# Two attention layers: copies of the turned weights shared out anew, and the split context kept in DRAM for the second layer

## What is computed

```python
x = x + _L0_xattn_ref(_layernorm(x), ctx_1024, ...)             # 16 heads of 16, biases
x = x + _L0_ffn_ref(_layernorm(x), ...)                         # top 2 of 8 experts
x = x + _L1_xattn_ref(_layernorm(x), ctx_1024, ..., mask)       # same context, other weights, a mask
x = x + _L1_ffn_ref(_layernorm(x), ...)
...
q = (x @ w_q).heads; k, v = (ctx @ w_kv).heads
out = softmax(q @ k.T * scale) @ v @ w_out
```

## Time and profile before

| | us |
|---|---|
| median of 3 timed runs | 782.3 |
| lowest, highest | 781.62, 786.86 |
| profiled execution | 776.57 |
| its span | 774.5 |

### The profile page before, as it was taken

One profiled execution on the slowest core, in us unless ns is written; L12 is line 12 of the kernel. 1 busy time (PEld: TensorE's weight loads), 2 busy tenths in 40 slices (PEclk: granted clock), 3 DMA queues, 4 the chain that ended last, 5 costly groups with the idle time before them and its releaser, 6 DMA issues. The chain is left out here.

```text
span 774.5 us, 14634 instructions
## 1 busy us (share of the span) xinstructions
PE 571.8 (74%) x5357; PEld 482.4 (62%) x5357; DVE 413.5 (53%) x1210; ACT 356.3 (46%) x816; POOL 147.8 (19%) x210
## 2 busy tenths in 40 slices
PE   4798999998448009999999940588889988827643
PEld 3676777776327009989899930476677777715432
DVE  3677677677421701343233253466656566648785
ACT  2676666666220004232232321357777777744520
POOL 1132333332100260000000055022323323100000
PEclk9899999999756558999999985789999999976978
DMA  5100000000198255554554213200000000000001
GB/s 150 58 15 8 22 22 2 2 1 2 31 347 270 86 186 204 184 198 154 187 191 157 75 58 106 88 22 22 8 16 21 2 2 2 2 2 1 0 1 47
DMA packets 38938, 57.11 MB, mean 74 GB/s; under 512 B 4410, under 2 KB 32083, under 8 KB 38740
## 3 DMA queue, kind: packets, MB, share of 16 engines
q1 hardware_dynamic: 37332, 52.50, 21.2%
q0 software_dynamic: 1536, 3.67, 1.5%
HBM read 47.91 MB, written 8.26 MB: 73 GB/s over the span
## 5 line engine op out<-in xcount | busy, mean ns | idle before, releaser
L788 PE MATMUL a_ring<-ident,a_e 112*125 112x112 f32 x768 | 102.2, 284 | 3.0 <-ACT a_e L411 3.0
L788 PEld LDWEIGHTS a_ring<-ident,a_e 112*125 112x125 f32 x768 | 90.7, 192 | 19.9 <-issue 14.8
L1118 ACT ACTIVATE ex_h_t<-ex_h,b_e 128x128 f32<-128x128 f32 x168 | 48.0, 369 | 97.9 <-PE ex_h L1370 97.9
L577 DVE CUSTOM_DVE_ANT_0 a_e<-a_s,a_mask 112x375 f32<-112x375 f32 x128 | 65.2, 542 | 39.3 <-issue 21.9
L1370 PE MATMUL ex_h<-ex_xg_t,w_s 128*128 128x128 f32 x672 | 80.9, 280 | 0.1
L1370 PEld LDWEIGHTS ex_h<-ex_xg_t,w_s 128*128 128x128 f32 x672 | 79.1, 197 | 0.5 <-DVE ex_xg_t L1265 0.5
L570 DVE TENSOR_REDUCE a_mx<-a_s 112x2 f32<-112x750 f32 x64 | 59.7, 933 | 32.7 <-PE a_s L779 32.7
L419 ACT ACTIVATE a_et<-a_ring 125x448 f32<-125x448 f32 x96 | 51.5, 536 | 53.1 <-PE a_ring L788 53.1
L411 ACT ACTIVATE a_e<-a_e,a_shift 112x375 f32<-112x375 f32 x128 | 70.4, 599 | 11.9 <-DVE a_shift L582 11.1
L1382 PE MATMUL ex_y<-w_s,ex_h_t 128*128 128x256 f32 x336 | 75.8, 379 | 0.0
L411 ACT ACTIVATE a_e<-a_s,a_shift 112x375 f32<-112x375 f32 x128 | 66.4, 571 | 12.5 <-DVE a_shift L582 12.2
(11 more groups left out here) (253 smaller groups left out, 849.9 us busy)
## 6 DMA issues: line engine op xcount, KB each, us to landing
w_s<-in_L_ffn_W SPq DMA_DIRECT2D x21, 1024.0 KB, 5.0
w_all<-in_L_ffn_W SPq DMA_DIRECT2D x8, 1024.0 KB, 11.9
a_ctx<-in_ctx SPq DMA_DIRECT2D x16, 375.0 KB
x_slots<-ex_zeros SPq DMA_DIRECT2D x1, 2688.0 KB
ex_xg<-x_slots SPq DMA_DIRECT2D x21, 128.0 KB, 4.9
y_slots<-ex_y_sb SPq DMA_DIRECT2D x21, 128.0 KB, 1.7
b_all<-in_L_ffn_b SPq DMA_DIRECT2D x1, 1024.0 KB
wu<-in_L_ffn_w SPq DMA_DIRECT2D x1, 1024.0 KB, 5.9
```

The source lines that it names most:

```text
L577: ins = v.tensor_tensor_reduce(out=es[:, t % 2, r, 0:SK], in0=s[0:S, r * 512:r * 512 + SK], in1=mask_sb[:], scale=1.0, scalar=-3.0e38, op0 ...
L788: last = nc.tensor.transpose(bank("et", t, kc)[0:KP, r * S:(r + 1) * S], es[:, t % 2, r, kc * KP:(kc + 1) * KP], ident[0:S, 0:S])
L1118: last = a.activation(h_t[:, i % 2, f], hb[i % 2][:, f * 128:(f + 1) * 128], ACT.Gelu, bias=b1_e[:, i % 2, f:f + 1])
```

## The change

1. In both layers ScalarE copies pieces 0 and 1 one after the other, ahead of all exponentials of the pass; VectorE copies piece 2. (Line numbers of the changed kernel are higher by 1 to 37.)
2. In layer one SyncE stores each batch's split context, 752 KB, into a new DRAM tensor `ct_dram` (`keep_context`), once the split is done; the load of batch b+3 stands behind it in SyncE's program. GpSimd's split of the next batch waits for that store.
3. Layer two no longer loads, turns, copies or splits the context. GpSimd issues a load of the kept split (`load_turned`) into one of two buffers of `a_ct`: batches 0 and 1 at the start of the layer, batch b+2 in its pass g3. The units `ct` leave the ring. Keys and values wait for the load.

```diff
+    ct_dram = nc.dram_tensor("ct_dram", (B, 128, 2 * DC * SKP), F32)
...
+                ct_bufs = 1 if first else 2
+                ct_all = sb(f"{tag}_ct", [128, ct_bufs, 2, DC, SKP], F32R)
...
+                order = [u for u in order if first or u[0] != "ct"]
...
+                        def keep_context(b):
+                            if b:
+                                sp.wait_ge(ct_lo, 2 * b)
+                            else:
+                                wait_read(sp, "ct", 0, 0)
+                                wait_read(sp, "ct", 0, 1)
+                                sp.wait_ge(filled, 3)
+                            sp.dma_start(ct_dram[b], ct_all[:, 0].rearrange("p i c n -> p (i c n)").bitcast(F32)).then_inc(ct_kept, 16)
...
-                        load_ctx(1)
-                        load_ctx(2)
-                        for b in range(B - 3):
-                            wait_filled(sp, "ct", b, 1)
-                            load_ctx(b + 3)
+                        if first:
+                            load_ctx(1)
+                            load_ctx(2)
+                            for b in range(B):
+                                keep_context(b)
+                                if b + 3 < B:
+                                    load_ctx(b + 3)
+                            sp.wait_ge(ct_kept, 16 * B)
...
                             wait_filled(pool, "v", b - 1, 1)
-                            g_.tensor_copy(ct[:, 0, c, 0:SK], ct_raw[:, c]).then_inc(ct_hi, 1)
+                            pool.wait_ge(ct_kept, 16 * b)
+                            g_.tensor_copy(ct_all[:, 0, 0, c, 0:SK], ct_raw[:, c]).then_inc(ct_hi, 1)
...
+                        def load_turned(b):
+                            if b >= 2:
+                                wait_filled(pool, "k", b - 2, 1)
+                                wait_filled(pool, "v", b - 2, 1)
+                            g_.dma_start(ct_all[:, b % 2].rearrange("p i c n -> p (i c n)"), ct_dram[b].bitcast(F32R))\
+                                .then_inc(ctx_in[b % 2], 16)
+
+                        if not first:
+                            load_turned(0)
+                            load_turned(1)
...
                             if g == 3 and b + 2 < B:
-                                context(b + 2, 0)
-                                context(b + 2, 1)
+                                if first:
+                                    context(b + 2, 0)
+                                    context(b + 2, 1)
+                                elif b >= 0:
+                                    load_turned(b + 2)
...
                             if 0 <= t < NQ:
                                 turned(t, 0)
+                                turned(t, 1)
                             if t + 1 < NQ:
                                 exps(t + 1, 0)
-                            if 0 <= t < NQ and mask is not None:
-                                turned(t, 2)
-                            if t + 1 < NQ:
                                 exps(t + 1, 1)
...
                             if 0 <= t < NQ:
-                                turned(t, 1)
-                                if mask is None:
-                                    turned(t, 2)
+                                turned(t, 2)
...
                         def wait_context(b):
-                            if b:
+                            if not first:
+                                pe.wait_ge(ctx_in[b % 2], 16 * (b // 2 + 1))
+                            elif b:
                                 pe.wait_ge(ct_lo, 2 * b)
```

More of the change, by code:

```diff
@@ L115, in attention_layer @@
                 k_raw = sb(f"{tag}_k_raw", [128, DC, SKP])
-                ctx_sb = sb(f"{tag}_ctx", [KP, 3, KC, D])
-                ct = sb(f"{tag}_ct", [128, 2, DC, SKP], F32R)
-                ct_raw = sb(f"{tag}_ct_raw", [128, DC, SK])
+                first = x_from is not None
+                if first:
+                    ctx_sb = sb(f"{tag}_ctx", [KP, 3, KC, D])
+                    ct_raw = sb(f"{tag}_ct_raw", [128, DC, SK])
+                ct_bufs = 1 if first else 2
+                ct_all = sb(f"{tag}_ct", [128, ct_bufs, 2, DC, SKP], F32R)
                 vx = sb(f"{tag}_v", [KP, 2, KC, H, 32])
@@ L156, in attention_layer @@
                 w_in = [sem(f"{tag}_w_in{i}") for i in range(4)]
-                ctx_in = [sem(f"{tag}_ctx_in{i}") for i in range(3)]
+                ctx_in = [sem(f"{tag}_ctx_in{i}") for i in range(3 if first else 2)]
+                ct_kept = sem(f"{tag}_ct_kept")
                 filled = sem(f"{tag}_filled")
@@ L351, in context @@
                             if b == 0:
-                                a.activation(ct[:, 0, c, 0:SK], bank("ct", b, c)[:, 0:SK], ACT.Copy).then_inc(ct_first, 1)
+                                a.activation(ct_all[:, 0, 0, c, 0:SK], bank("ct", b, c)[:, 0:SK], ACT.Copy).then_inc(ct_first, 1)
                                 return
@@ L439, in _ @@
                             weight(1, 0)
-                        act.wait_ge(filled, 3)
-                        context(0, 0)
-                        context(0, 1)
+                        act.wait_ge(filled, 3 if first else 2)
+                        if first:
+                            context(0, 0)
+                            context(0, 1)
                         if not transposed:
@@ L483, in _ @@
                                     keys(b + 1, 1)
-                            if g == 3 and b + 2 < B:
+                            if g == 3 and b + 2 < B and first:
                                 context(b + 2, 0)
@@ L531, in first_context @@
                             dve.wait_ge(ct_first, c + 1)
-                            v.tensor_tensor(ct[:, 1, c, 0:SK], bank("ct", 0, c)[:, 0:SK], ct[:, 0, c, 0:SK].bitcast(F32),
+                            v.tensor_tensor(ct_all[:, 0, 1, c, 0:SK], bank("ct", 0, c)[:, 0:SK], ct_all[:, 0, 0, c, 0:SK].bitcast(F32),
                                             ALU.subtract).then_inc(is_read("ct", 0, c), 1)
@@ L620, in _ @@
                         normal(0)
-                        first_context(0)
-                        first_context(1)
+                        if first:
+                            first_context(0)
+                            first_context(1)
                         if not transposed:
@@ L878, in _ @@
                             if g == 3:
-                                if b + 2 < B:
+                                if b + 2 < B and first:
                                     context(b + 2, 0)
```

9 lines of the change are left out of this document (6 added, 3 removed).

## The result

The changed kernel takes 739.3 us (median of 4 runs, 735.4 to 741.0); the kernel before, on the same chip, 782.0 us. The ratio is 0.944 (95%: 0.938 to 0.951). The profiled execution took 735.4, its span is 733.4 us, 41.1 less than the 774.5 of the earlier trace rows.

The account below looks back on a forecast made before the run. Steps were taken as bound by waits for four PSUM banks, the loop through ScalarE's exponentials, and TensorE's program order in layer two. Layer one -7.3, layer two -3.0, -7.0 and -11.0 sum to -28.3: median 754.0 us, 8-in-10 range 745 to 770.

Parts of the forecast that it names:

- Start of layer two: Layer two's keys start earlier without the context's turn and split, -3.9; weights landing 0.9 later make it -3.0 us.
- Wait for the load: Layer two's values wait 0.5 us per batch for the kept context, taken to land 5.05 us after issue.
- The cover of 4.55: Time in layer two between issue of the kept-context load and the values wanting it: 4.55 us.
- The forecast's case without a wait: Layer two's kept-context load takes an estimated 3.8 us, so values do not wait and the total is 2.5 us less.
- g1: Second of a batch's four score steps: 4.75 us forecast in layer one, 4.68 in layer two without a bank wait.
- Rival 1: Layer two's kept-context load lands late: 766 us in all, or 780 if it lands at 9.3; chance 0.18.
- Rival 3: Layer two's kept-context loads crawl at 60 GB/s, making the kernel slower than before: 816 us; chance 0.04.
- Steady batches of layer one: Five layer-one batches from 75 to 180 us: each 19.95 us against 21.15 through fewer bank waits, -6.0 in all.
- rival 2: ScalarE's longer loop takes layer one's gain: 774 us, or 761 if only the gain vanishes; chance 0.08.
- light steps: Layer one's four end steps without bank waits, which pay for ScalarE's loop of 4.64 us: +1.3 in all.
- First steps: Steps before the steady batches: layer one's seven -2.6 us; layer two's -7.0, with bounds of -3.5 and -8.
- Rival 4: The copies do not free banks as claimed, leaving only the removed context work, about -15: 767 us; chance 0.08.

Follow-up runs that it names:

- second execution: The changed kernel run and profiled again without an edit: 739.5 us, ratio 0.948 to the kernel before; profiled span 737.9 us.
- query_weights_first: The kernel before, with layer two's query weights load issued ahead of the context's instead of behind it: 777.7 us, ratio 0.997.
- context_ahead: The changed kernel, with one raw context of 375 KB loaded into an unread tile ahead of layer two's query weights: 747.0 us, ratio 0.960.
- split_context: The changed kernel, with each context load of layer one in two pieces of 112 and 13 partitions: 738.6 us, ratio 0.949.
- late_load: The changed kernel, with the six loads inside layer two's steps issued later, behind the scores of the next step: 760.2 us, ratio 0.969.
- copy_between: The changed kernel, with ScalarE's copy of piece 1 in layer one moved between its two pairs of exponentials: 750.5 us, ratio 0.961.
- copies_only: The kernel before, with the copies dealt out as in the changed kernel in both layers and nothing kept in DRAM: 757.9 us, ratio 0.968.

## Why the prediction was wrong, and where it was right

The forecast of 754.0 had the mechanisms of both parts right and sized several terms too small; 739.3 lies below its range. The lower end of the forecast's own range, 746, held no wait for the load, 4 us more from layer one, and a start of layer two of -3.9. The last of these failed in both executions, by 4.5 and 3.0 us. Layer one stayed within its 4 in the second execution and went 1.7 beyond them in the first, where its early steps had the full clock.

**Start of layer two, -3.0 against -8.4 and -6.9: the step that failed most.** I took the query weights' landing before, 7.4 us, as given, and added 0.9 for the two loads on the other queue. But the 7.4 was itself a wait: the context's load stood ahead of the weights, and the change removes it. They land in 3.0 us, 4.4 earlier where I had 0.9 later. query_weights_first, context_ahead and split_context show that from three sides. The row for it was in my hands, 118 GB/s at 0.34 of the engines; I used it as the slowest bound of the new load and not to ask who else was waiting behind the old one. The other half of the term, -3.9 for the context's turn and split, was right: context_ahead, whose weights come even later than before, still has the keys 0.8 behind the turn of the weights instead of 5.1. At the keys the two make -7.7, after 0.97 of waiting for the kept context that I had not counted; the remaining -0.7 comes behind the keys.

**Wait for the load, 0.5 per batch against 0 to 0.25.** From a gather of 3.3 us and 316 GB/s I had composed 5.4, from the 1 MB load 4.3, and taken 5.05; it is 4.4 to 4.8. The cover of 4.55 is 4.63. The forecast's case without a wait (-13.5 in five batches) came true with -13.6, in part by luck: g1 takes 4.52 where I had 4.68, which pays for g2 (5.27 for 5.21) and for the two steps in which the load is late. Rival 1 was near: there is no margin left, and late_load shows that a load issued later is paid for in full. VectorE did not hold up any issue: the six inside the steps take 0.56 to 0.64 us each. Rival 3 fell: the load moved up to 445 GB/s. (My argument against it, no window below 118 GB/s, was badly read: the earlier trace rows has one of 83, a mean over a window that the load does not fill.)

**Steady batches of layer one, -6.0 against -8.6.** g2 (5.20, now 5.27) and g3 (5.03, now 4.94) were right. g1 was given 4.75, TensorE's busy time, and takes 4.52. The weight-load rows show why, before and after:

```profile
88.44 0.98 PEld L36 LDWEIGHTS a_ring<-a_ct,a_wr 128*128 128x128 f32 x6 [0.35 <-issue]
```

```profile
159.87 0.99 PEld L36 LDWEIGHTS a_ring<-a_ct,a_wr 128*128 128x128 f32 x6
```

Before the change the weight loads for the keys of g1 stood idle for 0.35 us. The profile names no releaser; I read it as the wait for piece 1's bank, since the matmul row ahead of them (the gathering of the heads, 0.65 us, whose end is modelled) lies over the gap and makes it count as busy, and since copy_between, which frees the bank later, brings 4.81 back. In g0 the split ended by S+3.1 and not S+3.3: 4.70 for 4.97.

**ScalarE's loop, rival 2.** Rival 2 fell. The light steps take 4.42 for the 4.64 that I gave them:

```profile
172.38 0.98 ACT L453 ACTIVATE a_et<-a_ring 125x448 f32<-125x448 f32 x2 [1.42 <-PE a_ring L824]
...
173.26 1.96 ACT L445 ACTIVATE a_e<-a_s,a_shift 112x375 f32<-112x375 f32 x4
...
175.37 0.77 PE L815 MATMUL a_s<-a_kp,a_qz 32*112 32x376 f32 x12 [1.44 <-ACT a_e L445]
```

The second copy starts 0.44 behind the first (0.98 for both), not at S+1.97, so the exponentials start at S+2.31. And by then both shifts are there, so four exponentials run in 1.96 us where the earlier trace rows has 2.08 with a shift between them. The last such step, S30 to S31, takes 4.84 in this execution at a granted clock of 0.68 and 4.41 in the second at 1.00, which is the 0.4 between the two columns of the table.

**First steps.** In layer one copies_only gives -2.5 from S1 to S8 where -2.6 was forecast: right. The 2.4 us more of the profiled execution are the clock. In layer two -7.0 became -5.6 and -5.1, and S1 to S2 got longer, not shorter:

```profile
488.26:494.75 6.49, 6.49 (x37) 5.91 (x38) 4.52 (x23) 4.07 (x8) 0.07 (x1) 0.51 0.01 3
```

TensorE is busy in all of it at a granted clock of 0.51; before it was 6.04 us at 0.72. Eight of the ten executions that load a kept context show 6.4 to 6.6 here, the other two 5.20. One of these two is split_context, whose layer two is that of the changed kernel, and there S1 to S8 gains 6.9. So the -7.0 was about the right size, and what is missing goes with the clock of this step. TensorE had idled before it, 2.7 us for the shift; that this idling is why the clock is low was not tried.

**Parts in code that the change leaves alone.** From S31 to layer two's first instruction the fourteen executions need 282.9 to 289.8 us, whatever the kernel; -1.7 is within that scatter. The same holds for the end of the span (+1.3, +1.8; 103.2 to 105.5 us in all fourteen). They take from the profiled difference, or add to it, as much as one of the terms.

**Rival 4** (the copies do not do what they say) is refuted by copies_only.

## What to carry to other kernels

A landing time in a profile is not a property of the transfer: ask what stood ahead of it in its queue, and on how many engines that ran, before using it in the sum; a removed load gives back the waits of all that queued behind it. Where a bank or a buffer is released by an engine with a queue of its own, the order within that engine decides: the same copy 1.0 to 1.4 us later gave back 1.24 of 1.72 us. And the busy time of TensorE can lie over a short wait; look at the gaps between its weight loads too.

## What the runs showed of the hardware

- A load of 375 KB over 125 partitions ran at 0.34 of the DMA engines and 122 GB/s; the same bytes in two pieces of 112 and 13 partitions at 0.92 and 315 GB/s.
- It held back the 256 KB behind it. In layer two they landed in 7.4 to 11.9 us with it ahead (four executions) and in 3.0 to 4.4 without it (eight; a ninth had 7.6). In layer one they landed in 8.5 to 10.7 behind one piece (twelve executions) and in 4.9 and 5.7 behind two.
- A direct load of 752 KB from GpSimd's queue has its first packet some 1.3 us after its issue, ends its traffic at 4.0 to 4.5 and releases a waiting engine at 4.4 to 4.8; from SyncE's queue it releases at 4.1 to 4.35.
- The same step of the same kernel ran at a granted clock of 1.00 in one execution and 0.53 in another, for 1.4 us. A difference between two profiled executions can hold that much for no reason of the kernels.
